# Query and key parts of causal attention: two fp32r parts in place of three bf16 parts

## The reference

```python
h = _layernorm(x) * (1 + ca) + sa
qkv = (h @ w_qkv).reshape(B, S, 3, 16, 16)         # B, S = 4, 2048
Q, K = apply_rope(qkv[:, :, 0]), apply_rope(qkv[:, :, 1])
attn = einsum('bqhd,bkhd->bhqk', Q, K) * 16 ** -0.5 # float32
attn = softmax(where(causal, attn, -1e6))
out = einsum('bhqk,bkhd->bqhd', attn, V)
x = x + ga * (out @ w_proj + b_proj)
```

## Time and profile before

| | |
|---|---|
| median of 3 runs | 3483.62 us |
| profiled execution, its own time | 3484.02 us |
| its span, first to last instruction | 3482.3 us |
| mean granted clock of PE | 0.923 of 2.4 GHz |
| PE busy | 2957.4 us (85%) |
| DVE busy | 2632.0 us (76%) |
| ACT busy | 1561.0 us (45%) |
| POOL busy | 960.2 us (28%) |

### The profile page before, as it was taken

One profiled execution on the slowest core, in us unless ns is written; L12 is line 12 of the kernel. 1 busy time (PEld: TensorE's weight loads), 2 busy tenths in 40 slices (PEclk: granted clock), 3 DMA queues, 4 the chain that ended last, 5 costly groups with the idle time before them and its releaser, 6 DMA issues. The chain is left out here.

```text
span 3482.3 us, 71053 instructions
## 1 busy us (share of the span) xinstructions
PE 2957.4 (85%) x22532; PEld 1651.9 (47%) x22532; DVE 2632.0 (76%) x4836; ACT 1561.0 (45%) x2096; POOL 960.2 (28%) x1130
## 2 busy tenths in 40 slices
PE   5884489999998989999999995763799999799998
PEld 3553123332232323233233224553688888677777
DVE  4885888888888888988888905877577777566666
ACT  1442056666666666666666681110344444211111
POOL 1775001111011111111111114776222232333332
PEclk8997589999999999999999996665899999899999
DMA  2675302121112121112121005553545454322222
GB/s 67 184 214 156 83 17 52 50 51 40 44 47 56 46 55 37 45 46 55 47 55 41 21 9 142 176 157 135 161 158 160 153 161 151 116 91 90 90 90 73
DMA packets 385649, 315.60 MB, mean 91 GB/s; under 512 B 112364, under 2 KB 371928, under 8 KB 385368
## 3 DMA queue, kind: packets, MB, share of 16 engines
q1 hardware_dynamic: 373080, 278.44, 27.8%
q0 software_dynamic: 12288, 33.57, 2.9%
HBM read 194.27 MB, written 116.92 MB: 89 GB/s over the span
## 5 line engine op out<-in xcount | busy, mean ns | idle before, releaser
L871 ACT ACTIVATE probs<-ps_s 128x1024 f32<-128x1024 f32 (+3 forms) x1280 | 1077.9, 895 | 675.5 <-PE ps_s L1030 674.9
L895 DVE TENSOR_REDUCE piece_rest<-ps_m 128x1 f32<-128x512 f32 (+3 forms) x1344 | 799.8, 647 | 107.7 <-PE ps_m L1005 48.9
L895 DVE TENSOR_REDUCE piece_late<-ps_m 128x1 f32<-128x512 f32 (+2 forms) x960 | 586.6, 666 | 67.3 <-PE ps_m L1005 35.6
L851 POOL TENSOR_SCALAR_AFFINE_SELECT probs<-probs 128x256 f32<-128x256 f32 x512 | 205.6, 408 | 1550.7 <-ACT probs L871 1546.6
L1030 PE MATMUL ps_s<-q_st,k_st 50*128 50x512 bf16 (+7 forms) x5120 | 596.3, 347 | 36.4 <-issue 16.5
L1045 PE MATMUL ps_o<-probs,vs 128*32 128x512 f32 (+3 forms) x5120 | 605.2, 545 | 11.3 <-POOL probs L851 9.9
L996 PE MATMUL ps_m<-k_st,q_st 48*128 48x512 bf16 (+3 forms) x2560 | 451.2, 366 | 164.0 <-DVE piece_rest L895 78.5
L996 PEld LDWEIGHTS ps_m<-k_st,q_st 48*128 48x128 bf16 x2560 | 114.7, 93 | 784.7 <-DVE piece_rest L895 386.6
L1030 PEld LDWEIGHTS ps_s<-q_st,k_st 50*128 50x128 bf16 (+1 forms) x5120 | 224.4, 95 | 268.4 <-ACT probs L871 97.3
L1757 ACT ACTIVATE act_g<-ps_g 128x512 f32<-128x512 f32 x117 | 70.1, 599 | 280.2 <-PE ps_u L1849 280.2
L2041 ACT ACTIVATE act_g<-ps_g 128x512 f32<-128x512 f32 x96 | 57.2, 596 | 297.3 <-PE ps_u L2141 259.4
(11 more groups left out here) (223 smaller groups left out, 5168.0 us busy)
## 6 DMA issues: line engine op xcount, KB each, us to landing
qk_parts<-parts SPq DMA_DIRECT2D x128, 192.0 KB, 2.8
k_st<-qk_parts SPq DMA_DIRECT2D x768, 32.0 KB, 1.8
q_st<-qk_parts SPq DMA_DIRECT2D x768, 32.0 KB, 1.8
x_r<-expert_rows SPq DMA_DIRECT2D x39, 512.0 KB, 4.6
expert_made<-made SPq DMA_DIRECT2D x39, 512.0 KB, 2.9
x_in<-in_L_attn_x_dram SPq DMA_DIRECT2D x32, 512.0 KB, 4.7
v_ones<-v_out SPq DMA_DIRECT2D x64, 256.0 KB, 4.6
vs<-v_ones SPq DMA_DIRECT2D x64, 256.0 KB, 3.6
```

The costliest lines, as they stand in the source:

```text
L851: pool.affine_select(out=block_now, in_=block_now, compare_op=ALU.is_ge, fill=0.0, base=0, pattern=[[0, 2], [1, P]], channel_multiplier=-1 ...
L871: act.activation(probs[:, u % PSLOTS, 2 * pair:2 * pair + 2, j * P:ST], ps_s[:, pair, :, j * P:ST], ACT.Exp, scale=SCALE).then_inc(exp_don ...
L895: v.tensor_reduce(dst, ps_m[:, bank, 0:n * w].rearrange("p (n w) -> p n w", n=n), AX.X, ALU.max) \
```

## The change

q and k are kept in two parts of type fp32r (four bytes; PE takes such an operand in one pass with reduced precision) instead of three of bf16. A head's stack has three blocks of 16 rows, high-high, high-low and low-high, so that all products kept are in one matmul of 48 rows, or 50 with the two rows of the maximum, which are fp32r too. There is no second half: `scores` issues 4 matmuls a position in place of 8. The pieces for the maxima keep their count and shape and are fp32r products; the mask products stay bf16, into the same banks.

In the first stage ACT copies the transposed values to fp32r, DVE subtracts that and writes the second part directly; the second copy on ACT and the second subtraction on POOL are gone. The 8 stores of a step carry 256 KB each in place of 192 KB, the loads of a region are 12 of 64 KB in place of 24 of 32 KB. The fills of ones cover as many elements as before, of four bytes in place of two.

```diff
-QPART = (0, 0, 1, 0, 1, 2)
-KPART = (0, 1, 0, 2, 1, 0)
-HALVES = 2
+QPART = (0, 0, 1)
+KPART = (0, 1, 0)
-SPLIT = len(QPART) // HALVES
+SPLIT = len(QPART)
...
-        parts = sb("parts", [P, 2, 3, QC, ST], BF16)
+        parts = sb("parts", [P, 2, len(PARTS), QC, ST], F32R)
...
-                    sp.wait_ge(part3, (u + 1) * TPS + TPS)
+                    sp.wait_ge(part2, (u + 1) * TPS + 2)
...
-            def third(u, t, slot):
-                pool.wait_ge(part2, u * TPS + (t + 1))
-                pool.tensor_tensor(parts[:, slot, 2, :, t * P:(t + 1) * P], rest[:, t, :, :],
-                                   parts[:, slot, 1, :, t * P:(t + 1) * P], ALU.subtract).then_inc(part3, 1)
...
                 v.wait_ge(part1, n + 1)
-                v.wait_ge(part3, n + 1)
-                v.tensor_tensor(rest[:, t, :, :], ps_x[:, t % 2, :, :],
-                                parts[:, slot, 0, :, t * P:(t + 1) * P], ALU.subtract).then_inc(rest_done, 1)
+                v.tensor_tensor(parts[:, slot, 1, :, t * P:(t + 1) * P], ps_x[:, t % 2, :, :],
+                                parts[:, slot, 0, :, t * P:(t + 1) * P], ALU.subtract).then_inc(part2, 1)
...
-            def second(u, t, slot):
-                act.wait_ge(rest_done, u * TPS + (t + 1 + 2))
-                act.activation(parts[:, slot, 1, :, t * P:(t + 1) * P], rest[:, t, :, :], ACT.Copy) \
-                    .then_inc(part2, 1)
...
-        q_st = sb("q_st", [P, 2, HALVES, PAIRS, S], BF16)
-        k_st = sb("k_st", [P, 2, HALVES, PAIRS, S], BF16)
+        q_st = sb("q_st", [P, 2, PAIRS, S], F32R)
+        k_st = sb("k_st", [P, 2, PAIRS, S], F32R)
...
-        top = sb("top", [P, 2, P], BF16)
-        low = sb("low", [P, 2, P], BF16)
+        top = sb("top", [P, 2, P], F32R)
+        low = sb("low", [P, 2, P], F32R)
...
-                            row = z * HROWS + i % SPLIT * HD
-                            sp.dma_start(stack[row:row + HD, slot, i // SPLIT, :, cols], src[:, z, :, :]) \
+                            row = z * HROWS + i * HD
+                            sp.dma_start(stack[row:row + HD, slot, :, cols].bitcast(F32), src[:, z, :, :]) \
...
-                                            q_st[rows, slot, 0, a + i, qi * P:(qi + 1) * P],
-                                            k_st[rows, slot, 0, a + i, kt * ST:kt * ST + w], start=(i == 0),
+                                            q_st[rows, slot, a + i, qi * P:(qi + 1) * P],
+                                            k_st[rows, slot, a + i, kt * ST:kt * ST + w], start=(i == 0),
...
-                for half in range(HALVES):
-                    for z in range(2):
-                        rows = rows_of(z, half)
-                        last = pe.matmul(ps_s[:, pair, z, j * P:ST], k_st[rows, slot, half, pair, kc * P:(kc + 1) * P],
-                                         q_st[rows, slot, half, pair, qt * ST + j * P:(qt + 1) * ST],
-                                         start=(half == 0), stop=(half == HALVES - 1))
+                for z in range(2):
+                    rows = slice(z * HROWS, z * HROWS + SPLIT * HD + MROWS)
+                    last = pe.matmul(ps_s[:, pair, z, j * P:ST], k_st[rows, slot, pair, kc * P:(kc + 1) * P],
+                                     q_st[rows, slot, pair, qt * ST + j * P:(qt + 1) * ST], start=True, stop=True)
```

More of the change, by code:

```diff
@@ L101, in block_kernel @@
                                                    number + 0 * block_no]), (P, 1, 1, 1)), "plan_tables").ap()
-    qk_dram = nc.dram_tensor("qk_parts", (GROUPS, 2, 3, HG * HD, S), BF16, kind="Internal").ap()
+    qk_dram = nc.dram_tensor("qk_parts", (GROUPS, 2, len(PARTS), HG * HD, S), F32, kind="Internal").ap()
     v_dram = nc.dram_tensor("v_ones", (GROUPS * S, HG * VW), F32, kind="Internal").ap()
@@ L344, in qkv_stage @@
         part1 = sem("p1_part1")
-        rest_done = sem("p1_rest")
         part2 = sem("p1_part2")
-        part3 = sem("p1_part3")
         qk_stored = [sem(f"p1_qk_stored{i}") for i in range(2)]
@@ L379, in body @@
                             sp.dma_start(dst.rearrange("o n r t -> r (o n) t"),
-                                         parts[half * 64:half * 64 + 64, slot, :, c, :]) \
+                                         parts[half * 64:half * 64 + 64, slot, :, c, :].bitcast(F32)) \
                                 .then_inc(qk_stored[slot], 16)
@@ L406, in _ @@
             pool.sem_inc(sum_done, TPS)
-            pool.sem_inc(part3, TPS)
             def rstds(u):
@@ L432, in run @@
                         rstds(b * SPB + s + 1)
-                    if tile(t, 3):
-                        u, tt, slot, _ = tile(t, 3)
-                        third(u, tt, slot)
             steps_of(run, pool)
@@ L442, in _ @@
             v.sem_inc(rope_done, TPS)
-            v.sem_inc(rest_done, 2)
+            v.sem_inc(part2, 2)
             def stat(u, slot, turn):
@@ L541, in run @@
                         first(*tile(t, 2))
-                    if tile(t, 3):
-                        u, tt, slot, _ = tile(t, 3)
-                        second(u, tt, slot)
             act.wait_ge(const_init, 1)
@@ L578, in turn_qk @@
                 pe.wait_ge(sum_done, n + 1 + TPS)
-                pe.wait_ge(rest_done, n + 1)
+                pe.wait_ge(part2, n + 1)
                 for c in range(QC):
@@ L772, in store_max @@
                         at = h % 2 * HROWS + SPLIT * HD + row
-                        sp.dma_start(q_st[at:at + 1, slot, 0, h // 2, q0 * P:(q0 + nq) * P],
-                                     src[h * nq:(h + 1) * nq, l, :]).then_inc(max_in[slot][l], 16)
+                        sp.dma_start(q_st[at:at + 1, slot, h // 2, q0 * P:(q0 + nq) * P].bitcast(F32),
+                                     src[h * nq:(h + 1) * nq, l, :].bitcast(F32)).then_inc(max_in[slot][l], 16)
             def store_o(g, k):
@@ L840, in _ @@
             for z in range(2):
-                ones = k_st[z * HROWS + 32:(z + 1) * HROWS, 1, 0, :, :]
+                ones = k_st[z * HROWS + 32:(z + 1) * HROWS, 1, :, :].bitcast(F32)
                 pool.memset(ones.rearrange("p a t -> p (a t)"), 1.0).then_inc(pool_own, 1)
@@ L886, in _ @@
             for z in range(2):
-                ones = k_st[z * HROWS + 32:(z + 1) * HROWS, 0, 0, :, :]
+                ones = k_st[z * HROWS + 32:(z + 1) * HROWS, 0, :, :].bitcast(F32)
                 v.memset(ones.rearrange("p a t -> p (a t)"), 1.0).then_inc(blank, 1)
@@ L982, in turn_o @@
                 last.then_inc(m_done, 1)
-            def rows_of(z, half):
-                return slice(z * HROWS, z * HROWS + SPLIT * HD + (MROWS if half == 0 else 0))
             def pieces(unit, slot, turn):
```

1 line of the change is left out of this document (removed).

## The result

The changed kernel takes 3566.23 us (median of four runs, 3563.09 to 3568.29); the kernel before, beside it, 3484.42. The ratio is 1.0234, with an interval of 1.0217 to 1.0252: 82 us slower, where 34 us faster was forecast. The profiled execution took 3564.23 us, its span is 3562.5.

The account below looks back on a forecast made before the run. The prediction took the groups as bound by DVE's reductions plus gaps where PE is late. Terms of -20 + 11.5 - 5 - 10.5 - 2 - 5.5 - 4 + 1.5 = -34 us gave 3450 us, range 3375 to 3505.

Parts of the forecast that it names:

- a slack of 0.095: Groups, unmasked units: PE's answer loop of 1.164 us at full clock lies below the 1.259 that DVE needs.
- The answer's size: Pieces: an exposed fp32r product takes 0.11 us longer at full clock, 0.16 at half; opening +11.5 us over 72 units.
- Halves side by side: Groups: two fp32r score products run at once on the array's halves, so a full position's scores take 0.73 us.
- rival B: fp32r halves don't run side by side, or only in part: 3768 us fully serial, 3565 at 0.1 over the margin; chance 0.11.
- Relief of the gaps: Groups: shorter scores cut DVE's waits by 2.6 us a group before unmasked pieces and 1.2 before masked ones.
- Masked units: Groups: some 16 of 24 masked units a group pay 0.11 to 0.15 us for the longer answer, +2.0 a group.
- The turned maxima: Groups: DVE's 47.1 us of waits on them stay, hanging on PE's loop start and a DVE-PE chain.
- The last group: Final group, without pieces: shorter scores give back about half of ACT's 11.4 us idle, -5 us (0 to -11).
- The first stage: Projection: without POOL's third part xn ends sooner and a 0.76 us PE stall closes, -10.5 us (0 to -13).
- The hand-over: Between projection and attention: last stores sooner -2 us, 12 fewer loads on SP -5.5, longer fills of ones +1.5.
- The second region: Attention's start: the next region's halved loads are no longer late, so PE's wait of 4.15 us goes, -4 us.
- rival C: Groups: with fewer rounds PE's clock falls to half in places, +105 us, 3555 us; sign: clock not above 0.95; chance 0.07.

Follow-up runs that it names:

- experiment 6: The kernel before with the upper half of the columns of every value product left out, except at a block's first key position: 3417.87 us, ratio 0.9805.
- experiment 2: The changed kernel with only the products for the row maxima back in bf16, read from the fp32r stacks with step two; scores stay fp32r: 3442.54 us, ratio 0.9883.
- experiment 1: The kernel before with the second half of every score product left out, 4 score matmuls a position instead of 8: 3448.27 us, ratio 0.9898.
- experiment 7: The changed kernel with POOL's second subtraction put back in the first stage on spare tiles, its result unused: 3587.45 us, ratio 1.0288.
- experiment 5: The changed kernel with bf16 maxima products and the first 128 of 512 value columns moved ahead of the second unit, on most full positions: 3414.59 us, ratio 0.979.
- experiment 3: The changed kernel with value products cut into two column halves, one moved ahead of the second slot's unit: 3655.51 us, ratio 1.0482.

## Why the prediction was wrong

**The step that failed** is the reading of the unbroken run: "There DVE sets the pace", and from it "a slack of 0.095", by which an unmasked unit could answer 0.11 later and pay 0.015. DVE's 1.259 a unit was not its own pace, which is 1.207 (experiment 6), but half a loop of 2.49 (each of the two counts the tail of its last reduction in). A run with no idle time shown looked like a busy engine and was one that waited a little each time. Its leg one had no slack, since leg one has nothing in it but the answer and the reduction; and in leg two the longer unit delays the values on PE, a place that the working never looked at. I had priced the answer at 0.5 + 2.0 a group, 37.5 us in all. Taking it back gave 6.0 a group at full clock, 90 us, and 23 more in the groups in which the clock falls (experiment 2).

The other steps, against their terms:
- **The answer's size**, 0.11 at full clock: right, 0.50 against 0.39, taken from full-array rows. At half clock 0.19 where 0.16 was taken; the opening's units cost 0.197 x 72 = 14.2 in place of 11.5.

The Trainium skill ("TensorE: Matmul & The Clock Gate", Fast Weight Load) gave, by my estimate, 80 to 93 ns more for an exposed load. The 32 cycles in that estimate stand there as the theory for fp8, with some 2x as measured, so the estimate was on the high side of what the Trainium skill states. The loads of the pieces show 183 ns in the median here and 93 with bf16, and the rule's direction, against the change, was the right one: fp32r behaves as the Trainium skill has it for FP32.

- **Halves side by side** (rival B's first form): they are. Four score products of 512 columns show 0.63 us, less than the 0.73 forecast, and with a spacing of 0.217 a serial version would show 0.5 + 3 x 0.22 = 1.15.
- **Relief of the gaps**, priced at -2.6 and -1.2 a group, 57 in all: 36 us in experiment 1, last group included, 20.6 in experiment 2, whose scores are fp32r. Smaller than said, though it exists. That the slower weight load of the fp32r scores makes the difference between the two is not shown.
- **Masked units**, +2.0 a group: their waits grew by 52.5 us, 3.5 a group. The mask's products stand behind the slower piece, which is the likely reason; no run takes it alone.
- **The turned maxima**, whose 47.1 us were to stay: DVE waits 38.6 for them after, and 38.0 in experiment 2.
- **The last group**, -5: nothing came. ACT's wait for scores is 11.3 us against 11.4. PE in its turn waits for ACT to free a bank, 7.0 us where it waited 3.0. The waits of PE in the last group, before (first fence) and after:

```profile
PE ps_s L1030 <- ACT probs L871: 3.0, 10, 0.4
```

```profile
PE ps_s L1004 <- ACT probs L849: 7.0, 19, 0.6
```

Most of the time saved on the scores has become that wait. The same halving in bf16 (experiment 1) does shorten the last group, 75.9 us where it was 80.1, while with fp32r scores it takes 78.6 after and 79.6 in experiment 2, at clocks of 0.98 and 0.96. That ACT and PE form a loop of the same sort here, in which the longer fp32r answer eats the gain, is what the rows suggest; no experiment was made on it.
- **The first stage**, -10.5: the right mechanism, sized too low. DVE starts on the last part at 292.1 after and at 310.8 in experiment 7, 18.7 later, and the medians differ by 21. The stall of 0.76 was only the part of the delay that PE showed; on DVE the 64 xn take 17 us less (experiment 7).

The Trainium skill ("SBUF — State Buffer", who interferes with whom) says that the DVE operation and GpSimd's exclude each other for the whole instruction; by it the term stood, and the trace agrees both ways, 912 to 402 ns with POOL's operation gone and 1048 with it back.
- **The hand-over**, -2, -5.5, +1.5: the loads did take 5.5 less (2.68 + 2.76 against 5.48 + 5.57), the fills took 3.47 us each with four-byte elements too, so the +1.5 was 0 (it didn't follow from its own figure either: eight times 0.684 less 3.47 is 2.0, not 1.4). But from the end of the last part to the first piece it is 36.9 after and 38.0 before. The stores of 256 KB ate most of the rest: SP has issued the last of them 12.6 us after the last part where it was 8.7, the last eight taking 7.32 us to issue where they took 6.20, and over the stage such a store lands 3.9 us after its issue in the median, where 192 KB took 2.8. They were costed at 0, up to +10.
- **The second region**, -4: right, 3.8.
- **The clock** (rival C), a rival and not a term of the sum: it came true in small. The groups have 0.97 where they had 0.99, and 18 of the 92 us lie in groups in which it falls. The sign that I had given, above 0.95 in the groups, was met all the same.

So rival B gave the right time by luck: 3565 was its time for an answer 0.1 over the margin, 0.195 longer in all, and for halves that don't run side by side. The answer is 0.11 longer, the halves do run side by side, there was no margin, and the price of the answer comes through two different legs. The range of 3375 to 3505 leaned on the slack too, so the time fell outside it.

## What to carry to other kernels

When two engines hand a few buffers to and fro in a fixed order, write down the loop between two issues of the same instruction and add up its legs, before calling either engine the bound; a merged row without idle time doesn't prove that an engine is its own pace. A saving counts only in the leg where it is the longer side, and a latency on the hand-over counts in every leg that it is in. Keep the cheap kind of operand for the product that another engine waits for, give the saving kind to the product beside it, and then move work into the room that this leaves, no more of it than the leg has. And compare stretches at the same granted clock before a whole difference is put down to a loop: here 18 of 92 us lay in groups in which the clock had fallen.

## What the runs showed of the hardware

- fp32r products of 48 or 50 rows run two side by side on the halves of the array at the rate of bf16; what they cost is the weight load, 183 ns in the median against 93 for the pieces, 0.11 us on an exposed product at full clock and 0.19 at half (the kernels after and before).
- The upper halves of fp32r values, read as bf16 with a step of two elements, load and stream as contiguous bf16 does: 93 ns in the median for the load and 0.40 us for the pair of products, where contiguous bf16 has 93 and 0.39 (experiments 2 and 5, the kernel before).
- A fill of 4096 elements a partition on DVE takes 3.47 us for two-byte and for four-byte elements.
- A POOL subtraction of 128x512 beside a DVE normalisation of 128x256 makes the latter last 1048 ns in the median instead of 402 (experiment 7 and the kernel after).
- TensorE's granted clock can stay at the lower level while the engine is nearly always busy: 0.70 over the first group of experiment 3, with PE busy 129.2 of 136.8 us, after an opening at 0.50 with PE busy 63 of 117 us.
